# Four-layer graph network on one core: a four-word record for each pair of tiles in place of an eighteen-word record for each group of eight

## The chip, the cores and the metric

The kernel runs on one core of a Trainium2 chip. The metric is the device time of one execution in microseconds (us): the median of three runs is 8134.93 us, the runs lie between 8115.99 and 8168.47 us.

## What is computed

The reference is a network of four message-passing layers over one graph, 3,125 nodes and 100,000 edges, with 160 features a node (64 scalars and 32 vectors of three). Cut to what matters:

```python
h = jnp.maximum(_layernorm(x, axis=-1), 0.0)
x = x + layer0(h, edge_attr_3, edge_attr_64, ..., edge_index)
h = jnp.maximum(_layernorm(x, axis=-1), 0.0)
x = x + layer1(h, node_vec1, src, dst, edge_attr_4, edge_attr_10, ...)
h = jnp.maximum(_layernorm(x, axis=-1), 0.0)
x = x + layer2(h, edge_attr_4, ..., edge_index)
h = jnp.maximum(_layernorm(x, axis=-1), 0.0)
x = x + layer3(h, node_vec1, edge_attr_4, edge_attr_8, ..., src, dst)
```

In each layer the features of an edge's source node are gathered, multiplied by weights that a small network computes from the edge's attributes (layers 0, 1 and 3; layer 2 has none), and summed over the edges that end in the same node (`segment_sum`). Layer 0 sums over the other end.

## The kernel before

**Tiles, groups and bins.** The edges are sorted by the node into which they are summed. Nodes are taken in bins of 32, edges in tiles of 128 that belong to one bin each: 880 tiles, 110 groups of `GT` = 8, four pairs to a group. A preparation of about 1,100 us counts and ranks the edges and writes them in that order to DRAM.

**Layers 1 to 3** gather compactly: the sorted edges without the padding of the tiles make 782 columns of 128 edges. POOL gathers column after column from the node table into a ring of 16 places (`columns`, line 901 on; the gather itself is L920). It raises `arrived` once for every four columns that have landed (L896), and before it overwrites a place it waits until the tiles that read it are done (L917; the counts for this come from the table `release`, which POOL loads four at a time, L906). A tile reads one column of the ring, the one that holds its edges; which one is only known at run time.

**One step of the edge loop** works on a pair of tiles. On DVE (`edges`, L1532 on) it is `flush`, which adds the sums of the pair three steps back into the accumulators of two bins in `acc` (two instructions, L1495, the second waiting for the first), and `products` in layers 1 and 3, which multiplies the gathered features by the weights (four instructions, L1509 and L1512 in turn). In the third step of a group comes `select` as well (L1476, L1486), which compares keys for the next group. On PE a step is `weights` (L1891, layers 1 and 3), `sums` (L1915 and L1917; L1911 in layer 2), once a group the hidden layer (L1867 in layer 1, L1871 in layer 3) and a transpose (L1857). ACT scales the selection matrices (L1084) and applies the activation function (L1067).

**What is read at run time.** At the head of each group DVE loads a record from the table `guide` in SBUF into its registers (L1542): 8 numbers of bins, 8 places in the ring (already multiplied by the width `NF`) and 2 counts of half groups of columns to wait for, 18 words; in layer 2 only the 8 bins. PE loads the last 10 words in layer 2 (L1924). Layer 0 has another table, from which DVE loads 8 bins (L1538). Every load is one instruction that stands in the queue of its engine; the registers then address `acc` and the ring. Register arithmetic (line 99 is the helper `wait`, which adds up a semaphore's value) stands in the same queue. Line 109 is the loop: one turn holds two groups, the first two and last two groups of a layer stand outside it.

```python
_, record = nc.values_load_multi_w_load_instructions(
    guide[0:1, bass.ds(g * RECORD, RECORD if L.mlp and L.compact else GT)], engines=(DVE,), ...)
slots, need = record[GT:2 * GT], record[2 * GT:]
...
if 2 * u % HALF == 0:
    wait(dve, S["arrived"], need[2 * u // HALF])
```

`guide` begins at word 18,944 of a partition of `acc`, a multiple of 16; record g begins 18 g words further on. The order of the work is the order of the code on each engine; nothing reorders it.

Of the kernel before, what the change touches and what calls it, by code (L numbers as in the profile page):

```python
# [16 lines left out]
P = 128  # L17
# [9 lines left out]
GT = 8  # L27
# [42 lines left out]
RECORD = 2 * GT + 2  # L70
LAG_FL = LAG_SC + 1
HALVES = -(-COLS // HALF)
# [5 lines left out]
def is_static(v):  # L78
    return isinstance(v, int)
# [143 lines left out]
def gnn_program(nc, t):  # L223

    ctx = ExitStack()
    with ctx:
# [12 lines left out]
        guide_dram = nc.dram_tensor("tile_guide", (3, TCOLS * P), I32).ap()  # L239
# [31 lines left out]
        guide = acc[0:1, guide_at:guide_at + (GROUPS + 1) * RECORD].bitcast(I32)  # L271
        index_at = guide_at + (GROUPS + 1) * RECORD
# [83 lines left out]
        tile_id, tile_bin, tile_pad, column, passed = (carve(TCOLS) for _ in range(5))  # L356
        column_i = carve(TCOLS).bitcast(I32)
        tab = carve(TCOLS * 5).rearrange("p (c k) -> p c k", k=5)
# [71 lines left out]
        for names, where, each in (("bn mean h side", s_p[1:], BLOCKS), ("ht hts m tab", (s_p[1], s_p[3]), BLOCKS),  # L430
# [3 lines left out]
                                   ("gc3", by_column, in_lane[3]), ("arrived", by_column, HALVES), ("copied", by_column, -(-COLS // RING_COLS)),  # L434
# [16 lines left out]
        NODE_LOADS = 9  # L451
# [66 lines left out]
        def copy_tiles(eng, kind, part, c):  # L518

            for v in range(0, SPREAD // 2, GT):  # L520
# [12 lines left out]
        def _(sp):  # L533
# [92 lines left out]
            sp.dma_start(guide_dram[:, :], rows_i[2:5, :]).then_inc(s_written, 16)  # L626
# [15 lines left out]
            sp.wait_ge(s_written, 48)  # L642
# [4 lines left out]
            records = guide.rearrange("a (g r) -> a g r", r=RECORD)  # L647
            bins = guide_dram[0:1, :]
            at = GT - 2 * LAG_FL
            with nc.allow_non_contiguous_dma(reason="a record per group"):  # L650
                sp.dma_start(records[:, 0, 0:2 * LAG_FL], bins[:, 0:2 * LAG_FL]).then_inc(s_nodes_of, 16)
                sp.dma_start(records[:, 0, 2 * LAG_FL:GT], bins[:, 0:at]).then_inc(s_nodes_of, 16)
                sp.dma_start(records[:, 1:, 0:GT], bins[:, at:at + GROUPS * GT].rearrange("a (g r) -> a g r", r=GT)).then_inc(s_nodes_of, 16)
                sp.dma_start(records[:, :, GT:2 * GT], guide_dram[1:2, 0:(GROUPS + 1) * GT].rearrange("a (g r) -> a g r", r=GT)).then_inc(s_nodes_of, 16)
                for h in range(2):
                    sp.dma_start(records[:, :, 2 * GT + h],
                                 guide_dram[2:3, 0:(GROUPS + 1) * GT].rearrange("a (g r) -> a g r", r=GT)[:, :, HALF * h + HALF - 1]).then_inc(s_nodes_of, 16)
# [27 lines left out]
        def _(pool):  # L685
# [135 lines left out]
            for n in range(4):  # L821
# [66 lines left out]
                def landed_column(r, u, S=S):  # L888
# [286 lines left out]
        def _(dve):  # L1175
# [117 lines left out]
            def tiles(o):  # L1293
# [31 lines left out]
                link(dve.tensor_scalar(column_i, passed, float(COLS - 1), None, ALU.min))  # L1325
                link(dve.tensor_scalar(column_i, column_i, RING_COLS - 1, None, ALU.bitwise_and))
                link(dve.tensor_scalar(tab[:, :, 3], column_i, float(NF), None, ALU.mult))
                link(dve.tensor_scalar(column_i, passed, float(COLS - 1), None, ALU.min))
# [724 lines left out]
```

## Time and profile before

| | us |
|---|---|
| median of three runs | 8134.93 |
| runs, lowest and highest | 8115.99, 8168.47 |
| span of the profiled execution, first to last instruction | 5998.2 |
| median less span, which no row of the profile covers | 2136.7 |

The profiled execution has a page of its own and its time in full is not given there, only its span; so the span is set beside the median of the runs. In a page of a profile the engines are PE (matmul), PEld (its weight loads), DVE, ACT, POOL and SP; a name with q (DVEq, POOLq) is the engine's instruction queue, in which register instructions, loads of registers and waits run, which aren't counted as busy. `<-` names what a wait ended on; "issue" is time for which no releaser was found, such as an instruction that stands behind a load of registers.

The stages by the span's clock: preparation to 1,106 us, edges of layer 0 to 2,284, of layer 1 from 2,412 to 3,567, of layer 2 from 3,640 to 4,655, of layer 3 from 4,750 to 5,922, the end at 5,998; between them the node work of each layer.

### The profile page before, as it was taken

Reading aid. Unit: us, or ns where it says so; the run is one execution under the profiler, and the core shown is the slowest. Engines: PE = TensorE matmul, PEld = TensorE weight load, DVE = VectorE, ACT = ScalarE, POOL = GpSimd, SP = SyncE. Lnnn points to the kernel's source line nnn. Section 1 sums busy time; section 2 is a strip of 40 time slices with the busy share of each in tenths; the row PEclk is TensorE's granted clock in tenths of the full one; section 3 lists DMA queues with packets and bytes.
Section 4 is the critical chain, followed back from the end, with each engine's and each line's share of the span. In section 5 each row is a group of like instructions: output and inputs, shape, how many; then the busy total and the mean of one; then the engine's idle time right before and its main releaser. Section 6 shows DMA issues by size and latency. Waiting matters only on the chain.

```text
span 5998.2 us, 122036 instructions
## 1 busy us (share of the span) xinstructions
PE 4489.1 (75%) x24426; PEld 3923.9 (65%) x24427; DVE 3441.9 (57%) x11481; ACT 3414.1 (57%) x14717; POOL 4014.9 (67%) x4467
## 2 busy tenths in 40 slices
PE   7793121599999998788888886555555888888888
PEld 5552110588888888788888885444444877777777
DVE  8894000577777776566666664333333666666666
ACT  0000000366555554677777776677778677777775
POOL 6777777677777764676666646777777376666654
PEclk8896555799999999899999996555555899999999
DMA  8533333344444441222222212333333122222221
GB/s 307 181 80 74 80 79 82 77 88 88 87 88 88 88 87 36 71 73 70 68 68 65 64 48 69 77 78 77 78 79 79 44 74 70 68 67 64 64 62 41
DMA packets 643946, 484.25 MB, mean 81 GB/s; under 512 B 437482, under 2 KB 551593, under 8 KB 643707
## 3 DMA queue, kind: packets, MB, share of 16 engines
q0 software_dynamic: 181776, 292.84, 19.4%
q1 hardware_dynamic: 379563, 149.21, 10.3%
q10 hardware_dynamic: 82496, 40.92, 2.3%
q8 instruction: 45, 0.74, 0.1%
q14 instruction: 66, 0.54, 0.0%
HBM read 400.40 MB, written 96.88 MB: 83 GB/s over the span
## 4 chain that ended last, share of the span: by engine, by line
issue 28%; PE 22%; DVE 11%; DMA 9%; DVEq 6%; POOL 4%; ACT 1%; POOLq 1%; SPq 0%; ACTq 0%
DMA gath<-table,rows 6%; DVE acc L1495 5%; PE bank L1915 4%; PE bank L1891 4%; PE bank L1917 4%; PE bank L1867 3%; DVEq L1542 3%; PE bank L1911 2%; DMA gath<-table,small 2%; PE bank L1971 2%; DVE work L1512 2%; DVE work L1509 2%; POOL gath L920 2%; POOL gath L881 2%; DVE work L1529 1%
## 5 line engine op out<-in xcount | busy, mean ns | idle before, releaser
L920 POOL DMA_INDIRECT gath<-table,small x2346 | 2226.1, 949 | 1069.8 <-issue 611.7
L1084 ACT ACTIVATE sel<-acc,rows 128x32 f32<-128x32 f32 x10560 | 2292.6, 310 | 302.3 <-DVE acc L1486 247.6
L1495 DVE TENSOR_TENSOR acc<-acc,bank 128x160 f32 (+1 forms) x3520 | 1207.4, 343 | 1476.3 <-issue 583.1
L1915 PE MATMUL bank<-work,sel 128*128 128x160 f32 (+1 forms) x5280 | 1353.2, 339 | 342.4 <-DVE acc L1495 342.0
L1915 PEld LDWEIGHTS bank<-work,sel 128*128 128x128 f32 x5280 | 914.5, 196 | 420.0 <-DVE acc L1495 396.4
L1917 PE MATMUL bank<-work,sel 128*128 128x160 f32 x5280 | 1181.1, 306 | 0.0
L1891 PE MATMUL bank<-w,work 128*128 128x224 f32 (+2 forms) x5280 | 1153.8, 342 | 17.6 <-DVE work L1529 8.9
L881 POOL DMA_INDIRECT gath<-table,rows x880 | 832.0, 945 | 348.2 <-issue 196.2
L1891 PEld LDWEIGHTS bank<-w,work 128*128 128x128 f32 (+1 forms) x5280 | 915.7, 195 | 89.7 <-issue 52.1
L1917 PEld LDWEIGHTS bank<-work,sel 128*128 128x128 f32 x5280 | 937.8, 196 | 44.7
L752 POOL DMA_INDIRECT rows_a<-acc x782 | 754.6, 965 | 280.3 <-issue 237.5
L1911 PE MATMUL bank<-gath,sel 128*128 x1760 | 554.5, 491 | 450.6 <-POOLq L896 277.3
L1911 PEld LDWEIGHTS bank<-gath,sel 128*128 128x128 f32 x1760 | 454.3, 325 | 550.8 <-issue 550.8
L1067 ACT ACTIVATE work<-bank 100x512 f32<-100x512 f32 (+1 forms) x440 | 250.6, 596 | 786.3 <-PE bank L1871 283.8
L1084 ACT ACTIVATE sel<-sel,rows 128x32 f32<-128x32 f32 x2640 | 582.2, 308 | 124.6 <-DVE sel L1486 97.1
L1512 DVE TENSOR_TENSOR work<-bank,gath 128x192 f32<-128x192 f32 x1760 | 610.9, 347 | 0.0
L1509 DVE TENSOR_TENSOR work<-bank,gath 128x128 f32<-128x128 f32 x1760 | 499.8, 284 | 76.2 <-PE bank L1891 33.0
L1529 DVE TENSOR_TENSOR work<-bank,gath 128x288 f32<-128x288 f32 x880 | 357.1, 447 | 0.0
L997 ACT ACTIVATE acc<-acc 128x69 f32 (+1 forms) x34 | 9.2, 272 | 599.7 <-DMA acc<-in_rows_a 516.3
L1788 PE MATMUL bank<-acc,ident 100*128 100x391 f32 (+3 forms) x1000 | 347.7, 439 | 0.0
L1525 DVE TENSOR_TENSOR work<-bank,gath 128x256 f32<-128x256 f32 x440 | 185.2, 421 | 244.8 <-POOLq L869 244.7
L1716 PE MATMUL bank<-ident,sel 128*64 128x128 f32 x25 | 10.2, 407 | 396.3 <-ACT sel L980 396.3
(296 smaller groups left out, 3998.6 us busy)
## 6 DMA issues: line engine op xcount, KB each, us to landing
rows<-rows_b SPq DMA_DIRECT2D x330, 128.0 KB
gath<-table,small POOLq DMA_INDIRECT x2346
rows_a<-acc ACTq DMA_DIRECT2D x1, 30360.0 KB, 102.9
rows<-rows_a SPq DMA_DIRECT2D x110, 256.0 KB
acc<-in_rows_a SPq DMA_DIRECT2D x34, 793.5 KB
gath<-table,rows POOLq DMA_INDIRECT x880, 2.6
acc<-in_rows_b SPq DMA_DIRECT2D x34, 368.0 KB, 3.7
rows_a<-acc POOLq DMA_INDIRECT x782
```

The costliest lines, as they stand in the source:

```text
L752: pool.indirect_dma_start(rows_dram[0][:, :], bass.IndirectOffsetOnAxis(ap=pos_r[q][:, u:u + 1], axis=0), stage[0][q][:, u * A_W:(u + 1) * ...
L881: pool.indirect_dma_start(gath[q][:, u, :], None, table_dram[n][:, :], bass.IndirectOffsetOnAxis(ap=flat[:, u * w + first:u * w + first + ...
L920: pool.indirect_dma_start(gath_all[:, u, :], None, table_dram[n][:, :], bass.IndirectOffsetOnAxis(ap=index_r[q][:, u:u + 1], axis=0)).then ...
L1084: i = act.activation(sel[q][:, t, at:at + BIN], hot, ACT.Copy, scale=e[:, k:k + 1])
L1495: dve.tensor_tensor(sums, sums, bank(6 + b, P, 256 * h, 256 * h + L.width), ALU.add).then_inc(S["fl"].sem, 1)
L1509: dve.tensor_tensor(ps, wt[:, 0:128].rearrange("p (w c) -> p w c", w=2), one[:, 0:S0].unsqueeze(1).to_broadcast([P, 2, S0]), ALU.mult)
L1512: ins = dve.tensor_tensor(pv, wt[:, 128:L.wcols].rearrange("p (w m) -> p w m", w=nv) .unsqueeze(2).to_broadcast([P, nv, 3, V1]), one[:, S0 ...
L1529: ins = dve.tensor_tensor(pv, wt[:, h, 128:L.wcols].rearrange("p (w m) -> p w m", w=nv) .unsqueeze(2).to_broadcast([P, nv, 3, V1]), two[:, ...
L1891: ins = pe.matmul(bank(4 + u % 2, P, 224 * h, 224 * h + L.wcols), hid, w, start=True, stop=True, skip_group_check=True)
L1911: ins = pe.matmul(out, sel[qv][:, t, 0:128], gath_flat[:, bass.ds(slots[t], NF)] if L.compact else gath[qv][:, t, :], start=True, stop=Tru ...
L1915: pe.matmul(out, sel[qv][:, t, 96:224], work[:, a + NF:a + NF + L.width], start=True, stop=False, skip_group_check=True)
L1917: ins = pe.matmul(bank(6 + b, P, 256 * h, 256 * h + NF), sel[qv][:, t, 0:128], work[:, a:a + NF], start=False, stop=True, skip_group_check ...
```

## The change

The table `guide` now holds a record of four words for each pair of tiles: two bins and two columns. The column is the plain number from 0 to 781. Where the ring's place is needed, the engine works it out (`column & 15`, times `NF`), and where it waits for the column to have landed, it waits for `column + 1`, for which POOL now raises `arrived` with every column. DVE loads a record in every step of layers 1 to 3, PE in every step of layer 2. POOL masks the counts of `release` before it waits for them. The preparation computes four rows of the table in place of five, and the record is laid out when it is written to DRAM (three transfers for one), so that one transfer brings it back (for six).

```diff
-RECORD = 2 * GT + 2
+RECORD = 4
+RECORDS = (GROUPS + 1) * PAIRS
+TILE_MASK, COLUMN_MASK = 1023, 1023
...
-        guide = acc[0:1, guide_at:guide_at + (GROUPS + 1) * RECORD].bitcast(I32)
+        assert guide_at % (2 * GT) == 0
+        guide = acc[0:1, guide_at:guide_at + RECORDS * RECORD].bitcast(I32)
...
+        def pair_record(kind, i):
+
+            _, record = nc.values_load_multi_w_load_instructions(
+                guide[0:1, bass.ds(i * RECORD, RECORD)], engines=(kind,), min_val=0, max_val=COLS - 1,
+                skip_runtime_bounds_check_because="bins and columns of tiles")
+            bins = [nc.s_assert_within(v, 0, BINS - 1, skip_runtime_bounds_check_because="bins") for v in record[0:2]]
+            return bins + list(record[2:4])
+
+        def ring_column(column):
+
+            return gath_flat[:, bass.ds((column & (RING_COLS - 1)) * NF, NF)]
...
-            sp.dma_start(guide_dram[:, :], rows_i[2:5, :]).then_inc(s_written, 16)
+                sp.dma_start(records[:, 0:LAG_FL, 0:2], pairs_of[2:3, 0:LAG_FL, :]).then_inc(s_written, 16)
+                sp.dma_start(records[:, LAG_FL:, 0:2], pairs_of[2:3, 0:RECORDS - LAG_FL, :]).then_inc(s_written, 16)
+                sp.dma_start(records[:, :, 2:4], pairs_of[3:4, 0:RECORDS, :]).then_inc(s_written, 16)
...
+            sp.dma_start(guide, guide_dram[:, :]).then_inc(s_nodes_of, 16)
...
-                    last = is_static(r) and r * RING_COLS + u == COLS - 1
-                    pool.sem_inc(S["arrived"].sem if u % HALF == HALF - 1 or last else s_apart["pool"], 1)
+                    pool.sem_inc(S["arrived"].sem, 1)
...
-                            wait(pool, S["sc"] if n == 2 else S["prod"], free[h])
+                            wait(pool, S["sc"] if n == 2 else S["prod"], free[h] & TILE_MASK)
...
-                        if 2 * u % HALF == 0:
-                            wait(dve, S["arrived"], need[2 * u // HALF])
-                            dve.sem_inc(s_apart["dve"], 1)
+                        wait(dve, S["arrived"], (record[3] & COLUMN_MASK) + 1)
+                        dve.sem_inc(s_apart["dve"], 1)
...
-                            one, at = gath_flat[:, bass.ds(slots[2 * u + h], NF)], (2 * u + h) * L.row
+                            one, at = ring_column(record[2 + h]), (2 * u + h) * L.row
...
-                        if L.compact and n == 2:
-                            wait(pe, S["arrived"], need[v // 2])
-                            pe.sem_inc(s_apart["pe"], 1)
+                    if n == 2:
+                        wait(pe, S["arrived"], (columns[1] & COLUMN_MASK) + 1)
+                        pe.sem_inc(s_apart["pe"], 1)
```

Line 99 of the kernel before is line 102 of the changed one, L1495 is L1500, L1509 and L1512 are L1513 and L1516; L535 is the new load.

DVE in the loop of layer 1, before: the step from the first pair of a group to the second (REGISTER_ALU and ISA are register instructions, the second a fused address; TENSOR_TENSOR is the work).

```order
L1512 TENSOR_TENSOR work<-bank_4,gath 128x2x96
L99 ISA
L99 REGISTER_ALU [waits s_sc]
L1495 ISA [waits s_fl]
L1495 TENSOR_TENSOR acc<-acc,bank_67 128x160
L99 REGISTER_ALU
L1495 ISA [waits s_fl]
L1495 TENSOR_TENSOR acc<-acc,bank_67 128x160
L99 REGISTER_ALU
L1509 ISA [waits s_w_1]
L1509 TENSOR_TENSOR work<-bank_5,gath 128x2x64
```

The same place in the changed kernel:

```order
L535 ISA
L535 TENSOR_LOAD acc
L102 ISA
L102 REGISTER_ALU [waits s_sc]
L1500 ISA [waits s_fl]
L1500 TENSOR_TENSOR acc<-acc,bank_67 128x160
L102 REGISTER_ALU
L1500 ISA [waits s_fl]
L1500 TENSOR_TENSOR acc<-acc,bank_67 128x160
L102 REGISTER_ALU x2
L102 REGISTER_ALU [waits s_arrived]
L1513 REGISTER_ALU [waits s_w_1]
```

A load of registers with its address now stands ahead of every flush, and between the flush and the first product there are three more register instructions and, in this step, a wait for `arrived` that was not there; behind them come the address and the product, as before.

PE in the loop of layer 2, before: the second pair of a group.

```order
L99 ISA
L1911 ISA [waits s_fl]
L1911 MATMUL bank_67<-gath,sel_0 128x160
L1911 ISA
L1911 MATMUL bank_67<-gath,sel_0 128x160
```

The same pair in the changed kernel:

```order
L535 ISA
L535 TENSOR_LOAD acc
L102 REGISTER_ALU x2
L102 ISA [waits s_arrived]
L1912 REGISTER_ALU [waits s_fl]
L1912 ISA
L1912 MATMUL bank_67<-gath,sel_0 128x160
L1912 REGISTER_ALU
L1912 ISA
L1912 MATMUL bank_67<-gath,sel_0 128x160
```

The load of the group's record has left the head of the group, and each pair has a load, its own wait for `arrived` and a register instruction for each place in the ring.

## Rows read from the trace of the kernel before

**Rows 1.** The page: the span, and the granted clock in 40 slices

```profile
span 5998.2 us, 122036 instructions
PEclk8896555799999999899999996555555899999999
```

**Rows 2.** Edge loops of layers 1, 2, 3: length, busy PE, PEld, DVE, ACT, POOL, PEclk, DMA

```profile
2412.00:3567.00 1155.00, 1019.96 (x6317) 945.14 (x6318) 729.17 (x2830) 886.78 (x3822) 752.85 (x831) 0.98 0.27 68
3640.00:4655.00 1015.00, 560.24 (x1801) 460.37 (x1802) 346.39 (x1116) 756.69 (x3520) 753.52 (x832) 0.52 0.31 78
4750.00:5922.00 1172.00, 968.28 (x5864) 920.10 (x5865) 731.04 (x2825) 836.41 (x3687) 746.93 (x823) 0.94 0.26 67
```

**Rows 3.** Longest wait of DVE, 2,440 to 3,560 us (layer 1): us in total, times, longest

```profile
DVE acc L1495 <- issue: 205.4, 53, 3.9
```

**Rows 4.** Loads by line: DVE layers 1, 2, 3, layer 0, POOL; ns min/median/max, first, last start

```profile
L1542 DVEq TENSOR_LOAD <-acc x107: 1564/1587/4074, 2446.1 to 3557.7; - x107
...
L1542 DVEq TENSOR_LOAD <-acc x109: 595/1854/1873, 3659.3 to 4646.1; - x109
...
L1542 DVEq TENSOR_LOAD <-acc x108: 1564/2818/4074, 4757.1 to 5913.2; - x108
...
L1538 DVEq TENSOR_LOAD <-tile_bins_row x111: 594/598/854, 1112.1 to 2284.1; - x111
...
L906 POOLq TENSOR_LOAD <-tile_bins_row x47: 322/325/332, 2456.3 to 3535.9; - x47
```

**Rows 5.** Timeline of DVE in layer 1: start us, us, what [idle before]

```profile
2571.26 0.28 DVE L1509 TENSOR_TENSOR work<-bank,gath 128x128 f32<-128x128 f32 x1
...
2574.12 0.79 DVE L1495 TENSOR_TENSOR acc<-acc,bank 128x160 f32 x2 [1.85 <-PE bank L1917]
2574.91 0.29 DVE L1509 TENSOR_TENSOR work<-bank,gath 128x128 f32<-128x128 f32 x1
...
2575.85 0.77 DVE L1495 TENSOR_TENSOR acc<-acc,bank 128x160 f32 x2
2576.54 0.28 DVE L1509 TENSOR_TENSOR work<-bank,gath 128x128 f32<-128x128 f32 x1
...
2578.24 0.29 DVE L1509 TENSOR_TENSOR work<-bank,gath 128x128 f32<-128x128 f32 x1
...
2579.90 0.79 DVE L1495 TENSOR_TENSOR acc<-acc,bank 128x160 f32 x2
2580.61 0.28 DVE L1509 TENSOR_TENSOR work<-bank,gath 128x128 f32<-128x128 f32 x1
...
2585.49 0.78 DVE L1495 TENSOR_TENSOR acc<-acc,bank 128x160 f32 x2 [3.88 <-issue]
```

**Rows 6.** The chain of waits, loop end in layer 1, then a step of layer 3: start, us

```profile
2571.64 0.04 DVEq L109
...
2571.72 0.06 DVEq L109
...
2574.02 0.06 DVEq L1495
...
2574.12 0.33 DVE acc L1495
...
5032.02 0.02 DVEq L1503
...
5032.11 0.04 DVEq L99
...
5032.20 0.05 DVEq L1509
```

**Rows 7.** Timeline of PE in layer 3, behind a long load of DVE's

```profile
5022.07 0.90 PE L1915 MATMUL bank<-work,sel 128*128 128x160 f32 x2 [3.18 <-DVE acc L1495]
...
5023.30 0.74 PE L1915 MATMUL bank<-work,sel 128*128 128x160 f32 x2
...
5026.09 0.44 PE L1915 MATMUL bank<-work,sel 128*128 128x160 f32 x2
```

More of the change, by code:

```diff
@@ L69 @@
 RING_COLS = 2 * GT
-RECORD = 2 * GT + 2
+RECORD = 4
 LAG_FL = LAG_SC + 1
+RECORDS = (GROUPS + 1) * PAIRS
+TILE_MASK, COLUMN_MASK = 1023, 1023
+assert TILES <= TILE_MASK and COLS <= COLUMN_MASK
 HALVES = -(-COLS // HALF)
@@ L355, in gnn_program @@
         falls = carve(1)
-        tile_id, tile_bin, tile_pad, column, passed = (carve(TCOLS) for _ in range(5))
-        column_i = carve(TCOLS).bitcast(I32)
-        tab = carve(TCOLS * 5).rearrange("p (c k) -> p c k", k=5)
+        tile_id, tile_bin, tile_pad, passed = (carve(TCOLS) for _ in range(4))
+        tab = carve(TCOLS * 4).rearrange("p (c k) -> p c k", k=4)
         span, edge_i, some = carve(3), carve(3).bitcast(I32), carve(1)
@@ L450, in gnn_program @@
         s_fin = sem("s_fin")
-        NODE_LOADS = 9
+        NODE_LOADS = 4
+        WRITTEN = 5
         s_last = sem("s_last")
@@ L625, in _ @@
             sp.wait_ge(s_out_rows, 2)
-            sp.dma_start(guide_dram[:, :], rows_i[2:5, :]).then_inc(s_written, 16)
+            records = guide_dram.rearrange("a (i r) -> a i r", r=RECORD)
+            pairs_of = rows_i.rearrange("p (i h) -> p i h", h=2)
+            with nc.allow_non_contiguous_dma(reason="a record per pair of tiles"):
+                sp.dma_start(records[:, 0:LAG_FL, 0:2], pairs_of[2:3, 0:LAG_FL, :]).then_inc(s_written, 16)
+                sp.dma_start(records[:, LAG_FL:, 0:2], pairs_of[2:3, 0:RECORDS - LAG_FL, :]).then_inc(s_written, 16)
+                sp.dma_start(records[:, :, 2:4], pairs_of[3:4, 0:RECORDS, :]).then_inc(s_written, 16)
             sp.dma_start(first_node_dram.rearrange("(a c) -> a c", a=1), rows_f[1:2, :]).then_inc(s_written, 16)
@@ L646, in _ @@
             wait(sp, s_c[0]["trn"], BLOCKS)
[L647 to L657, printed above, removed]
+            sp.dma_start(guide, guide_dram[:, :]).then_inc(s_nodes_of, 16)
             sp.wait_ge(s_placed, 1)
@@ L1540, in edges @@
                             skip_runtime_bounds_check_because="counts of at most BINS bins, less one")
-                    else:
-                        _, record = nc.values_load_multi_w_load_instructions(
-                            guide[0:1, bass.ds(g * RECORD, RECORD if L.mlp and L.compact else GT)], engines=(DVE,), min_val=0,
-                            max_val=(RING_COLS - 1) * NF, skip_runtime_bounds_check_because="bins, places in the ring, counts of half groups")
-                        bins = [nc.s_assert_within(v, 0, BINS - 1, skip_runtime_bounds_check_because="bins") for v in record[0:GT]]
-                        slots, need = record[GT:2 * GT], record[2 * GT:]
                     for u in range(PAIRS):
-                        i = g * PAIRS + u
+                        i, record = g * PAIRS + u, None
+                        if n:
+                            record = pair_record(DVE, i)
                         if within(i - L.lag_fl, TILES // 2):
-                            flush(i, u, bins)
+                            flush(i, u, record[0:2] if n else bins[2 * u:2 * u + 2])
                         if L.mlp and within(i, TILES // 2):
-                            products(i, g, u, half, q, slots, need)
+                            products(i, g, u, half, q, record)
                         if u == 2 and within(g + 1, GROUPS):
@@ L1761, in rows_of_tiles @@
                 pe.wait_ge(s_tiletab, o + 1)
-                count = 5 if o else 1
+                count = 4 if o else 1
                 for c in range(TCOLS):
@@ L1910, in sums @@
                         if n == 2:
-                            ins = pe.matmul(out, sel[qv][:, t, 0:128], gath_flat[:, bass.ds(slots[t], NF)] if L.compact else gath[qv][:, t, :],
+                            ins = pe.matmul(out, sel[qv][:, t, 0:128], ring_column(columns[h]),
                                             start=True, stop=True, skip_group_check=True)
@@ L1921, in edges @@
                 def edges(g, half, q, n=n, L=L, S=S, turn=turn, hidden=hidden, weights=weights, sums=sums):
-                    slots = need = None
-                    if L.compact and n == 2:
-                        _, record = nc.values_load_multi_w_load_instructions(
-                            guide[0:1, bass.ds(g * RECORD + GT, GT + 2)], engines=(TENSOR,), min_val=0, max_val=(RING_COLS - 1) * NF,
-                            skip_runtime_bounds_check_because="places in the ring, counts of half groups")
-                        slots, need = record[0:GT], record[GT:]
                     for u in range(PAIRS):
@@ L1934, in edges @@
                         if within(i - L.lag_sc, TILES // 2):
-                            sums(i, g, u, half, q, slots, need)
+                            sums(i, g, u, half, q)
                         if L.mlp and within(g + 1, GROUPS):
```

34 lines of the change are left out of this document (15 added, 19 removed).

## The prediction

> **What bounds the kernel now.** I read the page first, then the busy times by stage, the waits, the instructions of the load's own line, and last the timeline of DVE over two groups. The span is 5998.2 us [rows 1]. The change touches the edge loops of layers 1 to 3, which take 1155, 1015 and 1172 us [rows 2]; layer 0 and the node work between the layers stay.
>
> Layers 1 and 3 gather the same 782 columns as layer 2 and yet take 140 and 157 us longer, so POOL's gathers aren't their bound. DVE is busy for only 63% there (729.17 of 1155), but its busy time leaves out what its queue does. Its longest wait in layer 1 is for nothing that the profile can name: 205.4 us in 53 pieces of up to 3.9 us, one in each turn of the loop (two groups) [rows 3]. The load of the record fills these holes. It takes 1.57 us in one group and 4.07 us in the next [rows 4]. The timeline shows DVE idle for 3.88 us ahead of the flush at 2585.49 and for 1.85 us ahead of the one at 2574.12; the releaser named there, PE, is no explanation, since the chain of waits goes through the load without a gap [rows 5, 6].
>
> So a turn can be added up from DVE alone [rows 5]. There are eight steps in it. From the first flush to the first product: 0.69 us without a wait for `arrived` (2575.85 to 2576.54), 0.79 with one (2574.12 to 2574.91), four of each: 5.92. From the first product to the next flush: 0.94 in an ordinary step (2574.91 to 2575.85, four of them), 1.66 with `select` (2578.24 to 2579.90, two), 4.88 with the long load (2580.61 to 2585.49), 2.86 with the short one and the loop's branch (2571.26 to 2574.12): 14.82. Together 20.74 us. The starts of the loads give as the mean of a turn (3557.7 - 2446.1) / 53 = 20.97 in layer 1 and (5913.2 - 4757.1) / 53.5 = 21.61 in layer 3 [rows 4]. DVE's queue, engine and loads alone explain layer 1 to 1%; layer 3 loses 0.64 more per turn. Where: behind a hole of 3.18 us PE's pairs of matmuls take 0.74 us, and 0.44 three microseconds later [rows 7]. The clock falls to its lower level in the hole; the stage's mean is 0.94, that of layer 1 0.98 [rows 2].
>
> **The price of the new load.** What a load costs hangs on its address. The record of group g begins 18 g words behind a multiple of 16, so even groups begin on a multiple of four words and odd ones don't. In layer 2 eight words from the same places take 0.60 and 1.86 us, in layers 1 and 3 eighteen words take 1.57 and 4.07 [rows 4]. Off the grid a word costs (4.07 - 1.86) / 10 = 0.22, which leaves some 0.10 fixed; on the grid eight words cost 0.598, so four cost (0.598 - 0.10) / 2 = 0.25 beside the fixed part: 0.35. All new records are four words on the grid. POOL loads just that, four words on the grid, in 0.325 us [rows 4]. It is another engine, so I take 0.34. The ends are 0.30 (half of DVE's eight words) and 0.598 (four as dear as eight).
>
> The Trainium skill, DMA: Bandwidth & Descriptors, section Latency and other measured facts, gives a load of registers a floor of about 600 ns; by it shorter records would buy nothing. Its figure matches the eight words of layer 0 (0.598), but POOL's four words at 0.325 lie well under it, so I treat it as a rival below.
>
> **The sum, part by part (layers 1 and 3, per turn).**
> Loads: two go, eight come, seven of them without a branch. In the ordinary handover I take the long one of before, 4.88 - 4.07 + 0.34 = 1.15, and add 0.09 for the ring's place that is worked out ahead of the third product: 1.24, five times: 6.20. Against the handover of before without a load (0.94) it adds 0.30 and not 0.45, because the queue runs ahead of the four products. With the branch: 2.86 - 1.57 + 0.34 + 0.09 + 0.03 (an address in two parts) = 1.75. With `select`, where the queue isn't ahead: 1.66 + 0.11 (address) + 0.34 + 0.03 = 2.14, twice: 4.28.
> Register instructions: between flush and product there come, beside what stands there in a step without a wait, two sums for the column, the wait and the ring's place. A plain one takes 0.08 (2571.64 to 2571.72), one at a wait 0.09 (5032.02, 5032.11, 5032.20), behind the last address the work starts after 0.10 (2574.02 to 2574.12) [rows 6]. That is 2 x 0.08 + 2 x 0.09 = 0.34, so 0.69 + 0.34 = 1.03, eight times: 8.24. This stands on the path: the product can't be issued before its address is there.
> Sum after: 8.24 + 6.20 + 4.28 + 1.75 = 20.47 against 20.74: 0.27 us less a turn. So 5.6 us of loads go and nearly as much comes back in small pieces.
> Layer 1: 53 x 0.27 = 14 us less. Layer 3: the holes that lower the clock are gone (the longest piece falls from 3.88 to some 0.3), so its 0.64 goes too: 53.5 x (0.27 + 0.64) = 49 less.
>
> **Layer 2.** PE loads four records a group for one and works out its addresses; per pair that is some 0.34 + 8 x 0.1 = 1.1 us of queue, and its pair has 1015 / 440 = 2.3 us. DVE's loads there go from 0.60 + 1.86 to 8 x 0.34 a turn, a wash, and DVE is busy for 346 of 1015. The gathers bound this layer (753.52 busy and their issue between them) [rows 2]. POOL's new mask, one for four columns, is computed while a gather runs. I cost all of it at nothing; without that cover the mask is 196 x 0.08 = 16 us a layer.
>
> **Smaller parts.** The finer wait lets the first pairs of a layer start up to two columns earlier, about 2 us each (a gather is 0.96, 753.52 / 782, and some 0.3 of issue): 6 us less over three layers. SP's five transfers fewer stand ahead of its wait for POOL's memset, and the three in the preparation have 1,000 us until they are needed: nothing; at worst 5 us. The preparation's shorter chain: under 1 us.
>
> **The sum.** 14 + 49 + 6 = 69 us less: the span goes from 5998 to 5929. The median is 2136.7 above the span, and nothing of the change stands in that part; I carry it over. 8134.9 - 69 = 8066 us.
>
> **The rivals.**
> (a) Slower: the load has a floor. If four words cost 0.598 like eight, each turn gains 8 x 0.26 = 2.07 us: layer 1 (2.07 - 0.27) x 53 = 95 more, layer 3 (2.07 - 0.91) x 53.5 = 62 more, with the starts 151: 8286 us. The change loses from the point where a load costs 69 / (8 x 106.5) = 0.08 more than I took, 0.42 us. For it speaks that DVE shows no load under 0.59; against it POOL's 0.325. Dearer still, if the rate of 0.22 a word held on the grid too: 0.98 a load, 0.64 x 8 = 5.1 a turn, 8610. The eight words at 0.598 speak against that.
> The Trainium skill, Runtime: NRT & Kernel Launch, section Instruction fetch mechanics, puts loads at about 200 ns a register even in bulk. The odd groups agree (0.22), the even ones (0.598 for eight) don't.
> (b) POOL becomes the bound: if the queue's small pieces all vanish behind products and flushes, layers 1 and 3 fall to layer 2's 1015: 297 less, 7838 us. Against it: in rows 5 and 6 each flush and product waits for its address already.
> (c) Layer 3 keeps its 0.64: PE is then idle more often, if for shorter, and its clock isn't back. 14 + 14 + 6 = 34 less, 8101 us. For it: in layer 2, where PE is busy for 55%, the clock is 0.52 [rows 2] and the slices show 5 [rows 1]. If that befell layer 3 wholly, PE's 968 us would become 968 x 0.94 / 0.52 = 1750, 580 us more; PE is busy for over 80% of both layers, so I give that 2 in 100.
> (d) The change doesn't do what it says: the loads aren't on the grid, or the waits by column release nothing earlier. The address of `guide` and of each record is a multiple of four words, so I count only the second, 6 us.
>
> **Chances and range.** Forecast, DVE's queue stays the bound and the gain is small: 0.70. (a) 0.11 with the dearer kind, (b) 0.06, (c) 0.11 and 0.02 for the clock that collapses. About what a measurement of this kernel can tell from no change is 1%, 81 us, and my 69 lie just inside. Of the forecast's own spread (a load of 0.30 gives 34 us more, register instructions at half their distance 60 more; a load of 0.40 takes 51) a little over half lies within it. So faster by over 1%: 0.36 + 0.06 = 0.42; within 1%: 0.34 + 0.11 = 0.45; slower: 0.13. Range: 7980 (the forecast with both gains is 7972) to 8150 (the dear load and 30 us of the others).
>
> **What would show it.** Right: DVE's loads all near 0.34 us, eight in a turn; a turn of 20.5 to 20.7 in both layers 1 and 3; no idle piece of DVE over 1 us; about 1.03 from flush to product; PE's pairs at 0.44 throughout in layer 3; layer 2 at 1010 to 1015. Wrong: loads at 0.6, a turn under 20.0 or over 21.0, a granted clock under 0.94 in layer 3, or more time in layer 2.

## The result, and the profile after

The changed kernel took 8259.4 us (median; 8227.8 to 8278.1) beside 8127.75 for the kernel before, a ratio of 1.0152 [1.0119, 1.0185]. I had forecast 8066, a gain of 0.8%; it lost 1.5%.

The page of the changed kernel, one of these executions: its span and the granted clock in 40 slices.

```profile
span 8226.3 us, 130699 instructions
PEclk7576755578888888888888989555555788888888
```

The span is within 2 us of the timed execution. That is the first surprise: the profile of before had a span of 5998.2 [rows 1], 2137 us below its median. The stages show where the difference sits. Layers 0, 1, 2, 3 of the changed kernel, by the starts of DVE's loads: length, then busy PE, PEld, DVE, ACT, POOL, granted clock, DMA share, GB/s.

```profile
1703.00:3367.00 1664.00, 1222.12 (x5900) 1074.19 (x5901) 876.60 (x2301) 691.05 (x2858) 825.58 (x874) 0.86 0.29 61
3496.00:5099.00 1603.00, 1220.45 (x6376) 1093.34 (x6376) 792.71 (x2856) 905.82 (x3850) 750.24 (x831) 0.86 0.19 49
5172.00:6484.00 1312.00, 621.62 (x1759) 429.36 (x1760) 343.51 (x1094) 800.80 (x3518) 745.51 (x822) 0.54 0.24 59
6568.00:8164.00 1596.00, 1147.58 (x5931) 1032.56 (x5932) 794.54 (x2856) 859.34 (x3741) 750.92 (x831) 0.85 0.19 49
```

Layer 0, which the change leaves alone, takes 1664 us where the profile of before has 1172. POOL is busy for as long as it was in layers 1 to 3 (750.24 us for 752.85 in layer 1, [rows 2]); what has grown is the time between its gathers, and TensorE's granted clock is 0.86 in layer 1 for 0.98. So this is another condition of the machine, and not a part of the time outside the stages. The experiments had to cover both. I call **A** the condition in which the median of the kernel before is 5997 to 6000 us, and **B** that in which it is 8128 to 8137. A batch of runs, each on one chip, came up in one or the other, and each ratio is to runs of before in the same batch.

### The profile page after: what moved, and what is told of

The parts are those of the page before. It is cut to its first block and busy times, and to the rows that moved or that the text cites. A ratio compares the mean times of both kernels' runs of the same rounds, so it can differ in the third digit from the quotient of the medians.

```text
span 8226.3 us, 130699 instructions
## 1 busy us (share of the span) xinstructions
PE 5088.6 (62%) x24426; PEld 4245.9 (52%) x24427; DVE 3574.1 (43%) x11476; ACT 3471.4 (42%) x14717; POOL 4004.5 (49%) x4467
## 3 DMA queue, kind: packets, MB, share of 16 engines
q0 software_dynamic: 181776, 292.84, 14.2%
## 5 line engine op out<-in xcount | busy, mean ns | idle before, releaser
L1500 DVE TENSOR_TENSOR acc<-acc,bank 128x160 f32 (+1 forms) x3520 | 1217.3, 346 | 2179.2 <-issue 867.4
L1890 PE MATMUL bank<-w,work 128*128 128x224 f32 (+2 forms) x5280 | 1332.7, 381 | 933.8 <-ACT work L1077 575.6
L1916 PE MATMUL bank<-work,sel 128*128 128x160 f32 (+1 forms) x5280 | 1489.3, 367 | 334.3 <-DVE acc L1500 248.7
L1890 PEld LDWEIGHTS bank<-w,work 128*128 128x128 f32 (+1 forms) x5280 | 1017.0, 216 | 1088.0 <-issue 672.5
L1918 PE MATMUL bank<-work,sel 128*128 128x160 f32 x5280 | 1269.9, 325 | 0.0
L1916 PEld LDWEIGHTS bank<-work,sel 128*128 128x128 f32 x5280 | 1008.8, 215 | 466.0 <-DVE acc L1500 354.9
L1918 PEld LDWEIGHTS bank<-work,sel 128*128 128x128 f32 x5280 | 1027.3, 214 | 57.8
L1912 PE MATMUL bank<-gath,sel 128*128 x1760 | 622.0, 496 | 692.3 <-issue 438.4
L1513 DVE TENSOR_TENSOR work<-bank,gath 128x128 f32<-128x128 f32 x1760 | 505.1, 287 | 712.0 <-issue 389.6
L1516 DVE TENSOR_TENSOR work<-bank,gath 128x192 f32<-128x192 f32 x1760 | 612.8, 348 | 38.3 <-issue 37.4
L1373 DVE COPY_PREDICATED acc<-work,bank 128x391 f32<-128x391 int16 (+3 forms) x500 | 253.4, 507 | 509.0 <-remote 349.3
L1072 ACT ACTIVATE attrT<-bank 128x256 f32<-128x256 f32 (+1 forms) x330 | 148.9, 451 | 682.4 <-remote 278.4
L1786 PE MATMUL bank<-work,acc 128*128 128x391 bf16 (+3 forms) x500 | 163.9, 328 | 429.0 <-issue 334.0
L1787 PE MATMUL bank<-acc,ident 100*128 100x391 f32 (+3 forms) x1000 | 400.4, 494 | 0.0
```

Of the source, the lines that this page charges most:

```text
L1500: dve.tensor_tensor(sums, sums, bank(6 + b, P, 256 * h, 256 * h + L.width), ALU.add).then_inc(S["fl"].sem, 1)
L1513: dve.tensor_tensor(ps, wt[:, 0:128].rearrange("p (w c) -> p w c", w=2), one[:, 0:S0].unsqueeze(1).to_broadcast([P, 2, S0]), ALU.mult)
L1516: ins = dve.tensor_tensor(pv, wt[:, 128:L.wcols].rearrange("p (w m) -> p w m", w=nv) .unsqueeze(2).to_broadcast([P, nv, 3, V1]), one[:, S0 ...
L1787: pe.matmul(out, ident[0:BINS, b:b + 1].to_broadcast([BINS, P]), base[o][0:BINS, lo:hi], start=False, stop=True).then_inc(s_prefix, 1)
L1890: ins = pe.matmul(bank(4 + u % 2, P, 224 * h, 224 * h + L.wcols), hid, w, start=True, stop=True, skip_group_check=True)
L1912: ins = pe.matmul(out, sel[qv][:, t, 0:128], ring_column(columns[h]), start=True, stop=True, skip_group_check=True)
```

## The experiments

Two theories at the outset. *Queue*: every register instruction, load and wait costs more in the timed executions than my rows said, so that the time goes by their number. *Apart*: the 2137 us lie outside the stages, and my sum fails for another reason. The later rivals place the loss: PE's queue in layer 2, DVE's loads, register arithmetic.

| run | kernel | condition | us | ratio to before |
|---|---|---|---|---|
| e1 | before, counts masked | B | 8155.7 | 1.0028 [1.0006, 1.0050] |
| e2 | e1, DVE's group loads aligned | B | 8064.4 | 0.9906 [0.9870, 0.9942] |
| e3, e9, e13 | after | B | 8256.5, 8266.4, 8257.8 | 1.0163, 1.0161, 1.0156 [1.0139, 1.0173] |
| e16 | after | A | 5920.2 | 0.9872 [0.9852, 0.9891] |
| e4 | after, DVE one load a group | B | 8216.3 | 1.0109 [1.0076, 1.0142] |
| e5 | after, PE one load a group | A | 5924.6 | 0.9880 [0.9865, 0.9895] |
| e10 | the same | B | 8191.3 | 1.0077 [1.0052, 1.0102] |
| e15 | after, both | B | 8121.0 | 0.9992 [0.9976, 1.0007] |
| e6 | e2, idle SP padded | A | 5751.9 (a fifth run 7779.6) | 0.9592 [0.9577, 0.9607] |
| e11 | the same | B | 8128.1 | 1.0005 [0.9986, 1.0024] |
| e7 | e2, masks on DVE | A | 5888.0 | 0.9819 [0.9805, 0.9832] |
| e12 | the same | B | 8107.5 | 0.9961 [0.9942, 0.9979] |
| e8 | e2, PE's load aligned too | A | 5747.2 | 0.9588 [0.9575, 0.9601] |
| e14 | the same | B | 8057.9 | 0.9909 [0.9892, 0.9925] |

**e1: the old structure under condition B.**

```diff
-wait(dve, S["arrived"], need[2 * u // HALF])
+wait(dve, S["arrived"], need[2 * u // HALF] & 255)
...
-wait(pool, S["sc"] if n == 2 else S["prod"], free[h])
+wait(pool, S["sc"] if n == 2 else S["prod"], free[h] & 1023)
...
-wait(pe, S["arrived"], need[v // 2])
+wait(pe, S["arrived"], need[v // 2] & 255)
```

> The kernel before, with a mask on the counts that POOL, DVE and PE wait for (two register instructions more per group on DVE, one per four columns on POOL, two per group on PE in layer 2). It gives a fresh profile of the old structure. Theory Q (the timed executions run with dearer queue instructions than the profile of before showed: each register instruction, load and wait costs more, so the time goes by their number): the span of its profile is near 8130 us and not 5998, all stages stretched, layer 0 included; the time is 8130 to 8170. Theory T (the 2136.7 us between span and median lie outside the stages, as my prediction took it): the span is again near 6000 and the time 8130 within 20 us.

The stages of e1, same columns and the same four layers as above:

```profile
1706.00:3371.00 1665.00, 1222.97 (x5899) 1078.76 (x5900) 879.43 (x2300) 689.97 (x2858) 824.94 (x873) 0.86 0.29 61
3500.00:5140.00 1640.00, 1225.95 (x6363) 1111.32 (x6362) 749.92 (x2848) 901.57 (x3850) 750.75 (x831) 0.85 0.19 48
5222.00:6431.00 1209.00, 566.21 (x1750) 449.07 (x1751) 338.37 (x1091) 808.23 (x3520) 740.42 (x817) 0.52 0.25 64
6517.00:8095.00 1578.00, 1117.45 (x5919) 1041.52 (x5920) 748.16 (x2851) 854.37 (x3741) 750.88 (x831) 0.84 0.20 50
```

The span is 8160.2: *Apart* falls, the whole kernel is stretched. The masks themselves cost 21 us by the medians, 0.3% in the table, so what follows is measured from a kernel that is a little slower than before. Against the four profiles of the changed kernel in B, the change takes some 30 us off layer 1 (1640 to between 1603 and 1618), adds some 20 to layer 3 (1578 to between 1595 and 1608) and some 100 to layer 2 (1209 to between 1308 and 1312). The loss is in the layer that I had costed at nothing. e3, e9 and e13 repeated the time of the changed kernel to 0.1%.

> The changed kernel as it is. Theory Q and every rival: 8240 to 8280 us, a ratio to before near 1.015. If instead the profile falls into an execution like that of before (span near 6000), its stages give the turn of 20.5 us that I worked out, and the loss is shown to lie only in executions whose queue instructions are dearer.

**e5, e10: PE's loads in layer 2.** PE loads the four records of a group at once and waits for columns once per half group.

```diff
-                        columns = pair_record(TENSOR, i)[2:4]
+                        columns = group[4 * u + 2:4 * u + 4]
...
-                    if n == 2:
-                        wait(pe, S["arrived"], (columns[1] & COLUMN_MASK) + 1)
+                    if n == 2 and v % 2 == 0:
+                        wait(pe, S["arrived"], (group[4 * u + 7] & COLUMN_MASK) + 1)
```

> The changed kernel, but PE in layer 2 loads the four records of a group with one load of sixteen words and waits for the columns once per half group, as before the change; DVE, POOL and layers 1 and 3 stay as changed. The profiles show that the change takes 25 to 38 us off layer 1, adds 17 in layer 3 and about 100 in layer 2 (1308 against 1210 us), where PE's longest waits are now for its own queue (422 us against 114). Theory PE2 (the loss is PE's queue in layer 2: eight loads, eight waits and their sums a turn for two loads): layer 2 falls to 1210 to 1250 us and the run to 8160 to 8210. Rival D2 (it is DVE's eight loads a turn in layer 2, or POOL's): layer 2 stays at 1290 or more, the run at 8240 or more. Theory Q by bare numbers (1,700 queue instructions fewer on PE at about 0.03 us): 50 us less, 8205.

> As e5_pe_group_layer2 (one load of the group's records on PE in layer 2). Where before runs at 8134, theory PE2 (the loss is PE's queue in layer 2): layer 2 at 1210 to 1250 us against 1308, the run at 8160 to 8210; rival D2 (DVE's eight loads): layer 2 at 1290 or more, the run at 8240 or more. Where before runs at 5997: 5920 to 5930 again.

In B layer 2 fell from 1308 (e9, the changed kernel in the same batch) to 1239 and the run by 75 us, as PE2 had it; in A nothing was to be had (5924.6 beside 5920.2 for the full change). PE's waits in layer 2 of the changed kernel in B (us in total, times, longest):

```profile
PE bank L1912 <- issue: 438.4, 194, 8.3
PE bank L1912 <- remote: 93.0, 15, 9.5
PE bank L1912 <- DVE acc L1500: 88.1, 79, 4.6
```

The same of e1, where the matmul is L1911:

```profile
PE bank L1911 <- DVE acc L1495: 241.6, 112, 11.5
PE bank L1911 <- remote: 176.2, 30, 12.9
PE bank L1911 <- issue: 114.0, 71, 8.1
```

Before, PE's longest wait was for DVE to free its bank; after, it is "issue", its own queue. ("remote" is a releaser that isn't in the trace. Traces of B lack more than half of the semaphore updates, so a single releaser there may be wrong; e10 is the stronger evidence.) POOL then waits for PE. POOL in layer 2, after in B:

```profile
POOL gath L930 <- PE bank L1912: 324.4, 80, 6.9
```

In e1:

```profile
POOL gath L920 <- PE bank L1911: 157.7, 48, 6.0
```

So the gathers, my cover for layer 2, weren't what bounded it in B, in part even before the change.

**e4, e15: DVE's loads.** One load of sixteen words a group on DVE, in layers 1 to 3; the arithmetic of the change stays. e15 has e5's edit beside it.

```diff
+            _, record = nc.values_load_multi_w_load_instructions(
+                guide[0:1, bass.ds(g * (PAIRS * RECORD), PAIRS * RECORD)], engines=(kind,), ...)
...
-                            record = pair_record(DVE, i)
+                            record = group[4 * u:4 * u + 4]
```

> The changed kernel, but DVE loads the four records of a group with one load of sixteen words at its head (aligned), and works out places and column counts as after. Three loads and three addresses fewer per group on DVE, the loaded words the same. By the rows 16 aligned words take about 1.4 us, four times four 1.36: in an execution without disturbance 8 us a layer either way, but the one long load stands in one piece before the first flush. Theory Q (number of queue instructions): 6 fewer a group, 1980 in three layers at 0.1 to 0.2 us each, so 100 to 200 us less than the changed kernel, 8060 to 8160. Rival A (register arithmetic between flush and product is what costs, the loads are not): within 30 us of the changed kernel, 8230 to 8290. Rival L2 (a long hole in DVE's queue is the dear thing): slower than the changed kernel by 50 us or more.

> The changed table and arithmetic with one load of sixteen words a group on DVE (e4) and on PE in layer 2 (e5, e10). Where before runs at 8134: if the two savings add up (40 on DVE, 70 on PE), 8150, with layer 2 at 1210 to 1230; if DVE's loads are what is left of layer 2's loss, layer 2 comes to 1210, as in the kernel before; if it is register arithmetic, it stays at 1235 or more. Where before runs at 5997: 5925 to 5945, since one long load stands in one piece ahead of the flush (1.1 us for 4 x 0.34, three addresses fewer).

e4 gained 40 us, between the rivals' numbers and short of *Queue*'s 100; 11 of them lie in layer 2 (1297 for 1308 in e3, of the same batch). e15 gained 137, more than 40 + 70, and its time is that of the kernel before. Its layer 2:

```profile
5174.00:6381.00 1207.00, 591.67 (x1750) 444.20 (x1751) 338.91 (x1092) 808.97 (x3515) 745.28 (x823) 0.52 0.25 64
```

That is e1's 1209 again, though the ring's places are still worked out as in the change. So the loss in layer 2 lies in what e5 and e4 take away together. Of some 100 us, PE's side is about 70 (e10). DVE's side is the other 32 (1239 to 1207), and nothing but loads and their addresses went there. What of PE's share is its loads and what its waits with their sums, no run parts. The number of instructions doesn't decide by itself, as *Queue* had it: e15 runs 127,444 for the 122,036 of before and takes the same time.

**e2, e8, e14: the group's record with every load on the grid of four words.** The table stays that of before, and so do e1's masks; in odd groups (`q` is 1) the load begins two words earlier.

```diff
+                        count = (RECORD if L.mlp and L.compact else GT) + 2 * q
...
-                            guide[0:1, bass.ds(g * RECORD, RECORD if L.mlp and L.compact else GT)], engines=(DVE,), min_val=0,
+                            guide[0:1, bass.ds(g * RECORD - 2 * q, count)], engines=(DVE,), min_val=0,
...
+                        record = record[2 * q:]
```

> As the run before, but DVE's load of the group's record begins two words earlier in odd groups, so that every load begins on a multiple of four words (18 and 20 words, 8 and 10 in layer 2). By the rows of before the long load falls from 4.07 to some 1.7 us, 2.3 us a turn: 53 x 2.3 = 122 us less in layer 1, and layer 3 to its floor of POOL's gathers, some 150 less. Theory Q: the same stalls go in the timed executions too, so the time falls by 150 to 270 us, to 7860 to 7980. Rival L (in the timed executions other stalls bound the turn, the long load is hidden): no change, 8110 to 8150.

> As e2_aligned_group, with PE's load in layer 2 begun two words earlier in odd groups too (10 and 12 words, all aligned). Theory PE2 (PE's queue is near the bound in layer 2): the long load goes from some 2.4 to 1.0 us in every second group, 55 x 1.4 = 77 us of queue, of which a third to all shows: 25 to 75 us less than e2, 7990 to 8040. Rival (layer 2 is bound by something else): 8050 to 8080.

> As e8_aligned_both. Where before runs at 8134: e2_aligned_group gave 70 us less than before with DVE's loads alone; with PE's aligned as well 8000 to 8064, nearer the upper end, since PE's load is one a group. Where before runs at 5997: 5747 again.

e8, layers 1, 2, 3:

```profile
2415.00:3465.00 1050.00, 1008.90 (x6364) 938.18 (x6363) 737.75 (x2850) 895.32 (x3850) 754.02 (x831) 0.99 0.30 75
3541.00:4541.00 1000.00, 538.88 (x1752) 444.51 (x1752) 339.33 (x1094) 755.69 (x3520) 746.14 (x823) 0.53 0.31 78
4628.00:5681.00 1053.00, 939.15 (x5922) 869.57 (x5922) 733.20 (x2851) 854.21 (x3741) 753.52 (x831) 0.99 0.30 74
```

The loads of the kernel before in layers 1 and 3 show how long these layers were:

```profile
L1542 DVEq TENSOR_LOAD <-acc x111: 1564/1970/4074, 2412.3 to 3577.5; - x111
L1542 DVEq TENSOR_LOAD <-acc x111: 1564/1583/4074, 4741.0 to 5932.6; - x111
```

In A this is the large gain: layer 1 goes from 1165 to 1050 us and layer 3 from 1192 to 1053, and the run is 4.1% shorter. In B DVE's aligned loads gave 0.9% (e2), 70 us, between the two theories: under the 150 of *Queue*, and clear of the rival's nothing. That the rest of the long load is hidden there behind other stalls is likely, but not shown. PE's aligned load on top gave nothing that can be told in B (0.9909 beside 0.9906), and layer 2 took 1219 us in e14, no less than e1's 1209: with one load a group PE's queue isn't near its bound, and the 25 to 75 us that I had expected rested on that. e8 and e14 are the best version found, ahead of both kernels in both conditions.

**e7, e12: register arithmetic by itself.** Four masks more in each step of layers 1 and 3.

```diff
-                        sums = acc[:, bass.ds(bins[2 * u + h] * L.width, L.width)]
+                        place = bins[2 * u + h] & 511 if L.mlp and L.compact else bins[2 * u + h]
+                        sums = acc[:, bass.ds(place * L.width, L.width)]
...
-                            one, at = gath_flat[:, bass.ds(slots[2 * u + h], NF)], (2 * u + h) * L.row
+                            one, at = gath_flat[:, bass.ds(slots[2 * u + h] & 4095, NF)], (2 * u + h) * L.row
```

> As e2_aligned_group, with a mask on each place in the ring and on each bin on DVE in layers 1 and 3, where the number is used: 16 register instructions more a group, 3,520 in all, four in each step. It prices register arithmetic on DVE, of which the change adds 31 a turn. By the rows of before 0.08 us each with half of them hidden: 0.16 a step, 70 us a layer, 140 in all if DVE is the bound in both layers, so 8200. Theory Q: the same or more, up to 0.1 us each, 350 us, 8415. Rival (DVE isn't the bound in these executions, since aligning its loads gave 70 of 270 us): under 50 us more, 8060 to 8110.

> As e7_dve_masks (four masks more in each step of DVE in layers 1 and 3). Where before runs at 5997: 5880 to 5895 again, 0.13 to 0.18 us a step. Where before runs at 8134: by theory P the same 140 us over e2_aligned_group or more, 8200 to 8300; if DVE isn't the bound in that condition, under 50 us more, 8060 to 8110.

In A they cost 5888.0 - 5747.2 = 141 us against e8 (136 against e6; e2 itself didn't run in A), 0.16 a step: the working that priced the change's arithmetic (0.08 for a plain one, half of them hidden) holds there, and DVE's queue is the bound. In B they cost 8107.5 - 8064.4 = 43 us, 0.05 a step, though e12 and e2 stood in different batches. There the rival holds: DVE's queue isn't the steady bound, though single instructions in it last up to 0.7 us.

**e6, e11: an idle engine's queue.** 24 semaphore increments more a group on SP, behind its transfer.

```diff
 sp.dma_start(rows_b(q).unsqueeze(1), src[:, bass.ds(g, 1), :]).then_inc(S[f"rows{q}"].sem, 16)
+for _ in range(24):
+    sp.sem_inc(s_apart["sp"], 1)
```

> As e2_aligned_group, with 24 semaphore increments more on SP behind each load of rows in layers 1 to 3 (7,900 queue instructions on an engine that is idle there, behind its transfer). Theory R (the executions share something among the queues of all engines, so that every queue instruction costs time wherever it stands; the stalls of 0.71 us come on one beat on DVE, PE and ACT): 80 to 250 us more than e2_aligned_group, 8145 to 8300. Theory P (only instructions in the path of DVE and PE cost): 8040 to 8090, as e2.

> As e6_sp_padded (7,900 semaphore increments on idle SP). Where before runs at 8134, theory R (in this condition the queues of all engines share something, and every queue instruction costs wherever it stands): 8145 to 8300; theory P (only those in the path of DVE and PE cost): 8040 to 8090. Where before runs at 5997: 5745 to 5760 again, no cost.

In A nothing (5751.9 beside 5747.2, with PE's load unaligned). In B the gain of e2 was gone: 1.0005 [0.9986, 1.0024] for 0.9906 [0.9870, 0.9942], 64 us by the medians, 8 ns for each of 7,920 instructions. The 8128.1 lie between the ranges of both theories. The padding in e11 (count, ns min/median/max, starts):

```profile
L611 SPq EVENT_SEMAPHORE  x7920: 1/17/1400, 3502.4 to 8029.1; - x198
```

And in e6:

```profile
L611 SPq EVENT_SEMAPHORE  x7920: 3/17/38, 2412.4 to 5667.9; - x198
```

Some of them last up to 1.4 us in B, where in A none lasts over 0.04. But it isn't so that nobody waits for them: SP's next transfer of rows stands behind them. DVE in layer 2 of e11:

```profile
DVE small L1478 <- DMA rows<-rows_b: 44.1, 22, 6.8
```

In the same layer of e2 and e14 DVE has no such wait, and in A (e6) there is none either. So part of the cost can be the late transfers. Layer 2 took 1225 us in e11, 1209 in e2 and 1218 in e14. Layer 3 has no such wait and still took 1571 us, beside 1546 and 1536. The executions stood in different batches. That in B a queue instruction costs time even where nobody waits for it is therefore likely by layer 3, and not shown.

**e16: the whole change in condition A.**

> The changed kernel as it is. Where before runs at 5997: 5928 by my sum, layer 2 at 1000 to 1015 us; PE2 (PE's queue over its bound there too): 5950 or more, layer 2 at 1030 or more. Where before runs at 8135: again 8240 to 8285.

Two earlier tries at this met condition B:

> The changed kernel as it is. The kernel before has run in two conditions by now: 8134 us beside e1 to e4 and 5997 us beside e5 to e8, the latter that of the profile shown ahead of the prediction. Where before runs at 5997: my sum for the undisturbed execution is 69 us less, 5928, with layer 2 at 1000 to 1015 us, layer 1 at 1147 and layer 3 at 1144 as in e5. Rival PE2 (PE's queue in layer 2 is over its bound there too): layer 2 at 1030 or more, the run at 5950 or more. Where before runs at 8134: again 8240 to 8285.

> The changed kernel as it is. Where before runs at 5997: 5928 by my sum, with layer 2 at 1000 to 1015 us; PE2 (PE's queue over its bound there too): 5950 or more, layer 2 at 1030 or more. Where before runs at 8134: again 8240 to 8285.

In e16 it came to 5920.2 beside 6000.4: 80 us less, 1.3%. The changed kernel in A, layers 1 to 3:

```profile
2408.00:3555.00 1147.00, 1086.74 (x6378) 934.59 (x6379) 785.25 (x2858) 906.26 (x3850) 751.28 (x831) 1.00 0.27 69
3627.00:4629.00 1002.00, 626.25 (x1757) 454.10 (x1758) 343.14 (x1097) 756.98 (x3520) 746.95 (x822) 0.50 0.31 78
4715.00:5859.00 1144.00, 995.62 (x5932) 868.26 (x5933) 784.98 (x2857) 853.95 (x3741) 750.56 (x831) 1.00 0.27 69
```

Its DVE in layer 1, start of a turn to the next (start us, us, what [idle before]):

```profile
2573.68 0.79 DVE L1500 TENSOR_TENSOR acc<-acc,bank 128x160 f32 x2 [0.27 <-PE bank L1918]
2574.70 0.29 DVE L1513 TENSOR_TENSOR work<-bank,gath 128x128 f32<-128x128 f32 x1 [0.23 <-POOLq L906]
...
2575.97 0.78 DVE L1500 TENSOR_TENSOR acc<-acc,bank 128x160 f32 x2 [0.25 <-issue]
...
2579.28 0.29 DVE L1513 TENSOR_TENSOR work<-bank,gath 128x128 f32<-128x128 f32 x1 [0.24 <-issue]
...
2581.41 0.32 DVE L1500 TENSOR_TENSOR acc<-acc,bank 128x160 f32 x1 [0.39 <-PE bank L1918]
...
2582.43 0.29 DVE L1513 TENSOR_TENSOR work<-bank,gath 128x128 f32<-128x128 f32 x1 [0.23 <-PE bank L1890]
...
2584.30 0.79 DVE L1500 TENSOR_TENSOR acc<-acc,bank 128x160 f32 x2 [0.84 <-PE bank L1918]
...
2594.38 0.78 DVE L1500 TENSOR_TENSOR acc<-acc,bank 128x160 f32 x2 [0.27 <-PE bank L1918]
```

## Why the prediction was wrong, by its own steps

**The step that failed** is in the sum: "The median is 2136.7 above the span, and nothing of the change stands in that part; I carry it over." The part isn't apart. In the executions that were timed every stage is longer, and the change puts 7.1% more instructions (130,699 for 122,036) into queues that stall there. The term of the sum that this breaks is layer 2, which I cost at nothing: it takes some 100 us more, and goes back when the loads of a group and PE's waits are put together again (e15). Layers 1 and 3, from which I had 63 us less, gave near nothing in B. A gap of 26% between span and time should have been a rival of its own: all my rows described another execution than the one that was to be forecast.

**Layer 2: nothing.** Right in A (from the first to the last matmul of the layer 997.3 us, before 997.4), wrong in B by some 100. My 1.1 us of PE queue for a pair against 2.3 was the margin of A alone. Here are PE's register instructions at the matmul of layer 2, after in A (count, ns min/median/max):

```profile
L1912 PEldq FUSED_REGOPS  x880: 46/46/51, 3631.3 to 4628.8; - x176
```

And in B:

```profile
L1912 PEldq FUSED_REGOPS  x880: 4/46/1393, 5175.4 to 6483.7; - x176
```

In B these and the loads stall in PE's queue: all that the trace has of its register instructions, loads and waits in layer 2 takes 342 us in A and 654 in B, and the cover, the gathers, didn't hold over that. In the trace of after in B, 487 of PE's register, wait and branch instructions in layer 2 last over 0.4 us, in e1 15, in e10 with a quarter of the loads 234. Their number alone isn't the loss: e15 has 271 and is as short there as e1.

**The four-word load: 0.34.** Right. DVE in layer 1 in A:

```profile
L535 DVEq TENSOR_LOAD <-acc x443: 339/344/640, 2408.4 to 3554.8; - x148
```

Rival (a), a floor at 0.598, falls with it; so does the floor of about 600 ns that the Trainium skill, DMA: Bandwidth & Descriptors, section Latency and other measured facts, gives.

**The turn: 20.47 from 20.74.** In A it measures 2594.38 - 2573.68 = 20.70. From flush to first product 1.02 (I had 1.03), ordinary handover 2575.97 - 2574.70 = 1.27 (1.24), with select 2581.41 - 2579.28 = 2.13 (2.14), with the branch 2584.30 - 2582.43 = 1.87 (1.75). The total is 0.23 over mine, as it was for the kernel before (20.97 by the loads, 20.74 by my sum), so the difference holds: by the starts of the loads in layer 1 the changed kernel's mean turn is (3554.8 - 2408.4) / 55.25 = 20.75, 0.22 less for the 0.27 forecast.

**Layers 1 and 3: 14 and 49 less.** In A, from the first to the last product of the layer, 18 and 48 less: layer 1 from 1153.8 to 1135.7, layer 3 from 1183.8 to 1136.2. The granted clock of layer 3 is 1.00 for 0.94 [rows 2]; rival (c) falls, in A. In B layer 1 gained some 30 and layer 3 lost some 20, and no term of mine accounts for either; that split isn't settled.

**The sum: 69 less.** In A 80 by the medians, 75 by the spans; short are layer 1 (14 forecast, 18 measured) and the starts with what lies between the layers (6 forecast, 9 by the spans). Rival (b), POOL as the bound, needed more than this change takes away: e8's layers 1 and 3 come within 50 and 53 us of its layer 2. One reading was off without touching the sum: by the first and last starts of DVE's loads the layers of before are 1165, 1001 and 1192 us long, and not 1155, 1015 and 1172; rival (b) would have been worth 354 us by that, and not 297.

**What stays open: the cause of B.** Some rivals go by the traces. It isn't slower work of the engines (DVE in layer 1 is busy for 792.71 us in B, 785.25 in A), nor TensorE's clock alone: layer 2 has a granted clock of 0.52 in A and in e1, and takes 1001 and 1209 us. Nor is it slower transfers: the packets of the largest queue took 19.4% of 5998.2 us in A (before) and 14.2% of 8160.2 in B (e1), nearly the same time. The chip isn't ruled out: A came up on chips 1 and 11, B on 6, 8 and 15, and no chip had two batches. Nor is a batch all of one kind: one run of e6 on chip 11 took 7779.6 us at a mean granted clock of 0.617, which is neither A nor B, and it has no trace.

The stalls of B come on a beat. e1, chain of waits in layer 2, where ACT's scalings follow each other (start us, us, what):

```profile
5808.11 1.10 issue
5809.21 0.32 ACT sel L1084
5809.53 0.40 issue
5809.92 0.32 ACT sel L1084
5810.24 1.08 issue
5811.32 0.32 ACT sel L1084
```

The distances are 0.71 and 1.40 us, one beat and two. In the trace of the changed kernel DVE's and PE's stalled queue instructions mostly last 0.70 and end on the same beat as each other. Records point to something shared: the traces of B hold about 45,000 updates of semaphores and 27,000 landings, those of A 112,000 and 88,000, for the same work. The Trainium skill, NOTIFIC — the notification-queue block, section 7.1, says that a full record queue may drop records or stall the engine that produces them, and that its inner pipeline always holds back. The missing records and the beat fit that, and it would make B a cost of recording. No run here shows it: every execution was recorded. Whether B would stretch an execution that isn't recorded can't be said.

## What to carry to other kernels

Set the profile's span beside the timed executions before anything else. Here the two lie within 3 us of each other when they are of one execution; the 2137 us between them meant that the profile was of another condition, and its rows gave only the sum for that one. In the other, added loads and waits in an engine's queue are the first thing to suspect. A load of registers paid for its alignment more than for its length here: put the record on a grid of four words and load it once, and leave its layout as it is (e8: 4.1% and 0.9%, where the change that was made gave 1.3% and lost 1.6%). An edit costed at nothing because another engine hides it is hidden only in the condition in which the rows were taken.

## What was new about the hardware

Loads of registers on DVE from SBUF, in A: four words 0.344 us; in e8, from an address that is a multiple of four words, eight words 0.60, ten 1.07, eighteen 1.57 and twenty 1.35. DVE in layer 1 of e8, eighteen and twenty words in turn:

```profile
L1543 DVEq TENSOR_LOAD <-acc x111: 1348/1571/1912, 2414.6 to 3465.1; - x111
```

Twenty words cost less than eighteen. These times fit an estimate of 0.25 for four words on the grid, 0.22 to 0.24 for a loose word and 0.09 fixed (0.09 + 4 x 0.25 + 2 x 0.24 = 1.57; 0.09 + 5 x 0.25 = 1.34). The 4.07 us of before fits eighteen loose words. Rounding the record up to a multiple of four words made its load cheaper.

The other surprise is that one kernel takes 5997 or 8135 us from one batch of runs to the next, each within 0.6% of its median, and that a change can gain 1.3% in the one and lose 1.6% in the other.
